# Order of the gate and up parts, and where the expert loop reads its bounds: a mixture-of-experts kernel on one core

## The reference, cut to what matters

```python
x = x + xattn(layernorm(x), ctx, ctx, mask, ...)
h = layernorm(x)                            # 2048 tokens x 256
shared = (silu(h @ gw) * (h @ uw)) @ dw     # 256 -> 512 -> 256
logits = h @ gate_w                         # 2048 x 32
id = argmax(logits); score = sigmoid(max(logits))
xs = (h * score)[argsort(id)]               # tokens sorted by expert
g = ragged_dot(xs, routed_gate_w, tokens_per_expert)
u = ragged_dot(xs, routed_up_w, tokens_per_expert)
d = ragged_dot(silu(g) * u, routed_down_w, tokens_per_expert)
out = x + shared + d[inverse order]
```

## Time and profile before

| | |
|---|---|
| median of 3 executions | 301.97 us (300.6 to 305.56) |
| the profiled execution, its own time | 302.95 us |
| its span | 301.0 us |
| granted TensorE clock, mean | 0.98 |
| PE busy | 255.7 us (85%) |
| DVE, ACT, POOL busy | 154.7, 94.2 and 88.5 us |
| HBM read, written | 59.49 MB, 8.91 MB |
| the expert loop, first to last gate matmul | 131.0 to 265.5 us |
| its gate and up matmuls (L1022) | 2528, 89.9 us busy |
| its down matmuls (L1044) | 1264, 50.5 us busy |

### The profile page before, as it was taken

How to read it: one execution, slowest core, us unless ns; L and a number is a source line. 1 busy time by engine, 2 the same in 40 slices (tenths; PEclk the granted TensorE clock), 3 DMA queues, 4 the chain that set the end, 5 groups by cost and what they waited for, 6 DMA issues and landing times.

```text
span 301.0 us, 13003 instructions
## 1 busy us (share of the span) xinstructions
PE 255.7 (85%) x4627; PEld 181.5 (60%) x4629; DVE 154.7 (51%) x490; ACT 94.2 (31%) x284; POOL 88.5 (29%) x248
## 2 busy tenths in 40 slices
PE   4977899998798999979797999899899899799710
PEld 3745656653383468747676787777787677553600
DVE  0538867884399341135454555555455455433423
ACT  2048766533121011433232333333233333212000
POOL 1245211111007766012122222222222222102772
PEclk9999999999799999999999999999999999999995
DMA  6999994000001234406989499999999999924565
GB/s 197 340 371 373 375 371 174 0 3 2 0 0 71 105 107 139 139 2 217 337 288 306 154 349 315 346 382 382 375 375 383 382 374 374 316 56 106 166 210 164
DMA packets 53040, 68.69 MB, mean 228 GB/s; under 512 B 3967, under 2 KB 35100, under 8 KB 53020
## 3 DMA queue, kind: packets, MB, share of 16 engines
q1 hardware_dynamic: 46203, 61.60, 59.1%
q0 software_dynamic: 1536, 4.20, 4.5%
q10 hardware_dynamic: 5280, 2.62, 3.4%
HBM read 59.49 MB, written 8.91 MB: 227 GB/s over the span
## 4 chain that ended last, share of the span: by engine, by line
PE 66%; DVE 9%; DMA 7%; issue 7%; POOL 5%; ACT 4%; POOLq 1%; ACTq 1%; SPq 0%; DVEq 0%
PE bank L1022 25%; PE bank L947 14%; PE bank L1044 12%; PE bank L959 5%; POOL xs_flat L463 4%; DMA ring_gu<-n_L_ffn_routed_up_w_dram 3%; PE bank L878 3%; DMA slot_rows<-late 2%; DVE h_place L531 1%; PE bank L913 1%; DVE h_place L532 1%; ACT h_place L746 1%; DMA h_place<-in_L_xattn_kernel_q_dram 1%; DMA xs_flat<-slot_rows,slot_i 1%; PE bank L896 1%
## 5 line engine op out<-in xcount | busy, mean ns | idle before, releaser
L1022 PE MATMUL bank<-ring_gu,x_c 128*32 128x128 f32 x2528 | 89.9, 276 | 9.7 <-issue 6.1
L1022 PEld LDWEIGHTS bank<-ring_gu,x_c 128*32 128x32 f32 x2528 | 64.0, 109 | 28.0 <-issue 15.7
L1044 PE MATMUL bank<-ring_d,h_place 128*32 128x128 f32 x1264 | 50.5, 274 | 3.9 <-issue 0.8
L644 DVE TENSOR_TENSOR h_place<-h_place,bank 128x128 f32<-128x128 f32 x79 | 22.7, 288 | 48.8 <-ACT h_place L781 48.8
L456 POOL COPY x_c<-xs_flat 128x32 f32 x79 | 16.7, 212 | 97.2 <-PE bank L1022 84.7
L1044 PEld LDWEIGHTS bank<-ring_d,h_place 128*32 128x32 f32 x1264 | 35.1, 109 | 11.5 <-issue 10.6
L781 ACT ACTIVATE h_place<-bank 128x128 f32<-128x128 f32 x79 | 21.9, 278 | 46.4 <-PE bank L1022 45.3
L786 ACT COPY late<-bank 128x128 f32 (+1 forms) x79 | 21.0, 266 | 45.3 <-PE bank L1044 45.3
L648 DVE STREAM_TRANSPOSE h_place<-h_place 128x128 f32<-128x128 f32 x79 | 24.6, 312 | 13.5 <-PE bank L1044 8.3
L959 PE MATMUL bank<-shd,h_place 128*128 128x256 f32 x128 | 28.4, 380 | 2.1 <-DVE h_place L532 2.1
L531 DVE SCALAR_TENSOR_TENSOR h_place<-h_place,bank 128x512 f32<-128x512 f32 x16 | 11.0, 686 | 34.0 <-ACT h_place L746 34.0
(11 more groups left out here) (132 smaller groups left out, 251.2 us busy)
## 6 DMA issues: line engine op xcount, KB each, us to landing
ring_gu<-L_ffn_routed_gate_w_dram SPq DMA_DIRECT2D x32, 512.0 KB, 8.9
ring_gu<-n_L_ffn_routed_up_w_dram SPq DMA_DIRECT2D x32, 512.0 KB, 10.1
ring_d<-L_ffn_routed_down_w_dram SPq DMA_DIRECT2D x32, 512.0 KB, 10.2
slot_rows<-late ACTq DMA_DIRECT2D x10, 256.0 KB, 5.9
x<-in_x_dram SPq DMA_DIRECT2D x4, 512.0 KB, 7.0
slot_rows<-zeros SPq DMA_DIRECT2D x1, 2048.0 KB, 14.3
late<-sorted_rows SPq DMA_DIRECT2D x8, 256.0 KB, 3.2
out_dram<-x SPq DMA_DIRECT2D x8, 256.0 KB, 2.4
```

Source lines behind the costliest of these rows:

```text
L644: v.tensor_tensor(h_r, g_silu, bank[1][:, 0:P], ALU.mult).then_inc(h_ready, 1)
L1022: ins = te.matmul(bank[g][q * LW:(q + 1) * LW, 0:P].rearrange("p (m f) -> p m f", f=LW), x_c[:, k], columns[:, q], start=(k == 0), stop=(k ...
L1044: ins = te.matmul(bank[2][r:r + LW, 0:DH], hT[:, f * LW:(f + 1) * LW], ring_d[:, s, f, a * DH:(a + 1) * DH], start=(m == 0), stop=(m == HA ...
```

## The change

Three things. In `gate_up` both gate parts come first, so that `g_done` is counted after the second part and not after the third; up's first part, with `x0_used` behind it, is now the third, and its wait for `h_ready` goes with it. The wait for half 1 of the tokens (`x1_part`) comes ahead of the second part rather than the third. The tables `turn_end` and `turn_first` become one table `turn` of unsigned 16-bit values, read without a check of bounds. And the round is rotated: the first chunk of the next expert stands at the end of an expert's piece, so that the loop over rounds is entered with a first chunk already done and with its number and end carried in two registers. `turn_first` and the `If` are gone.

```diff
-        turn_first = sb("turn_first", [1, NE], I32)
-        turn_end = sb("turn_end", [1, NE], I32)
+        turn = sb("turn", [1, NE + 1], U16)
...
-            v.tensor_scalar(turn_end[:], chunk_cum[0:1], 1.0, None, ALU.add).then_inc(table_ready, 1)
-            v.scalar_tensor_tensor(out=turn_first[:], in0=chunk_cum[0:1], scalar=1.0, in1=chunk_f[0:1],
-                                   op0=ALU.add, op1=ALU.subtract).then_inc(table_ready, 1)
+            v.memset(turn[:, 0:1], 1).then_inc(table_ready, 1)
+            v.tensor_scalar(turn[:, 1:NE + 1], chunk_cum[0:1], 1.0, None, ALU.add).then_inc(table_ready, 1)
...
                 part(0, 0)
+                pe.wait_ge(x1_part, w)
+                part(0, 1).then_inc(g_done, 1)
                 pe.wait_ge(h_ready, w)
                 part(1, 0).then_inc(x0_used, 1)
-                pe.wait_ge(x1_part, w)
-                part(0, 1).then_inc(g_done, 1)
                 part(1, 1).then_inc(u_done, 1)
...
-            def expert(w, e, s, before, landed):
-
-                pe.wait_ge(gu_in[s], 2 * landed)
-                gate_up(w, s)
-                end = pe.value_load(turn_end[0:1, bass.ds(e, 1)], min_val=2, max_val=MAX_CHUNKS + 1)
-                if before is None:
-                    with pe.If(it > 0):
-                        down_of(w, RING - 1)
-                else:
-                    down_of(w, before)
+            def turn_of(e):
+                return nc.values_load(turn[0:1, bass.ds(e, 1)], engines=(mybir.EngineType.PE,), min_val=1, max_val=MAX_CHUNKS + 1,
+                                      skip_runtime_bounds_check_because="unsigned, a running sum of chunks with at least one for each expert")
+
+            def other_chunks(w, end, s, landed):
+
                 pe.wait_ge(d_in[s], landed)
                 with pe.If(w + 1 < end):
                     with pe.Fori(w + 1, end) as more:
                         gate_up(more, s)
                         down_of(more, s)
                     pe.nop()
-                return end
-
+
+            def next_expert(w, e, s, landed):
+
+                n = (s + 1) % RING
+                pe.wait_ge(gu_in[n], 2 * landed)
+                gate_up(w, n)
+                end = turn_of(e + 2)
+                down_of(w, s)
+                return w, end
...
+            pe.wait_ge(gu_in[0], 32)
+            gate_up(1, 0)
+            carry(1, turn_of(1))
             with pe.Fori(0, ROUNDS) as it:
-                w = pe.value_load(turn_first[0:1, bass.ds(RING * it, 1)], min_val=1, max_val=MAX_CHUNKS)
+                w, end = carried()
                 for s in range(RING):
-                    w = expert(w, RING * it + s, s, s - 1 if s else None, 16 * it + 16)
-            w = pe.value_load(turn_first[0:1, RING * ROUNDS:RING * ROUNDS + 1], min_val=1, max_val=MAX_CHUNKS)
+                    other_chunks(w, end, s, 16 * it + 16)
+                    w, end = next_expert(end, RING * it + s, s, 16 * it + (16 if s + 1 < RING else 32))
+                carry(w, end)
+            w, end = carried()
```

More of the change, by code:

```diff
@@ L12 @@
 U32 = mybir.dt.uint32
+U16 = mybir.dt.uint16
 P = 128
@@ L1066, in expert, with carried, carry @@
                     pe.nop()
-                return end
+            def next_expert(w, e, s, landed):
[5 more added lines that the diff above has]
+                return w, end
+            first_turn = pe.alloc_register("first_turn")
+            first_end = pe.alloc_register("first_end")
+            def carried():
+                return (pe.snap(first_turn, min_val=1, max_val=MAX_CHUNKS),
+                        pe.snap(first_end, min_val=2, max_val=MAX_CHUNKS + 1))
+            def carry(w, end):
+                pe.reg_mov(first_turn, w)
+                pe.reg_mov(first_end, end)
+            pe.wait_ge(gu_in[0], 32)
+            gate_up(1, 0)
+            carry(1, turn_of(1))
             with pe.Fori(0, ROUNDS) as it:
-                w = pe.value_load(turn_first[0:1, bass.ds(RING * it, 1)], min_val=1, max_val=MAX_CHUNKS)
+                w, end = carried()
                 for s in range(RING):
-                    w = expert(w, RING * it + s, s, s - 1 if s else None, 16 * it + 16)
-            w = pe.value_load(turn_first[0:1, RING * ROUNDS:RING * ROUNDS + 1], min_val=1, max_val=MAX_CHUNKS)
+                    other_chunks(w, end, s, 16 * it + 16)
+                    w, end = next_expert(end, RING * it + s, s, 16 * it + (16 if s + 1 < RING else 32))
+                carry(w, end)
+            w, end = carried()
             for s in range(REST):
-                w = expert(w, RING * ROUNDS + s, s, s - 1 if s else RING - 1, 16 * ROUNDS + 16)
+                other_chunks(w, end, s, 16 * ROUNDS + 16)
+                if s + 1 < REST:
+                    w, end = next_expert(end, RING * ROUNDS + s, s, 16 * ROUNDS + 16)
             down_of(n_chunks + 1, REST - 1)
```

## The result

| | before | after |
|---|---|---|
| median of 20 runs each, us | 301.95 (300.6 to 305.56) | 300.2 (297.96 to 307.17) |
| ratio | | 0.9932, 95% interval 0.9907 to 0.9958 |
| profiled execution, us | 302.95, span 301.0 | 298.73, span 296.8 |
| loop's first load of gate, us into the span | 130.96 | 130.04 |
| SyncE issues expert 12's gate | 171.70 | 168.89 |

The medians differ by 1.75 us (0.6%), the ratio gives 0.7%. The forecast was 295.8 and the range began at 292.5 and ended at 300.0; the time lies just above it.

A forecast was written before the change was run, and what follows sets the result against it. TensorE's freeing of ring places bounds the loop's first half, the weight stream the second. Savings of 4.7, 2.1 and 0.3 us, taken as 7.0, gave 295.95 for the profiled execution, 295.0 at the median, stated as 295.8; range 292.5 to 300.

The forecast's parts named there:

- Expert 4's, without the pause inside it: First chunk of expert 4 in the loop's first half: saves 0.6 us, its 1.76 us pause staying as it is.
- the instruction pause moves: Rival, chance 0.12: the 1.76 us mid-chunk pause may not occur in code of another length, giving 294 us.
- expert 12's gate 4.7 us earlier: Sum of TensorE's savings up to the 23rd chunk, for which SyncE waits: expert 12's weights land 4.7 us earlier.
- the last up weights 6.8 earlier: End of the loop's weight stream: 4.7 us from the first half plus 2.1 us of stream pauses recovered.
- Chunks inside an expert: Chunks behind another of their expert take 1.35 us; eight of fifteen save 0.10 each, 0.8 us in all.
- the copies come late: Rival, chance 0.17: POOL's half 0 is released a part later, every chunk pays up to 0.13 us more: 298 us.
- First chunks of experts 1 to 3: First chunks of 1.96, 1.89 and 1.87 us become 1.46 through the unchecked read, saving 1.3 us.
- The ends of the round: Rotated round, at experts 5 and 6: two first chunks of 3.36 and 1.88 us become 1.53 and 1.96, saving 1.75.
- The first silu: Start of the loop: the first silu starts a part earlier and the 2nd chunk waits for it, saving 0.2 us.
- the pauses of the stream behind expert 12's gate: Transfers from 171.0 to 191.6 us: of 2.8 us of pauses waiting for experts 7 and 8, 2.1 go.
- the 17 us that TensorE alone would save: TensorE's savings over 79 chunks, about 17 us, ten of them waited away in the stream-bound second half.
- the clock's rival: Chance 0.05: TensorE's clock falls to half while it waits in the second half, slowing the last twelve experts: 311 us.

The follow-up runs named there:

- e6: Changed kernel with the ring's first refill of weights held until the 12th chunk's up is done: 305.29 us, ratio 1.0164 to the kernel before.
- e10: Kernel before with only expert 7's refill held until the 9th chunk's up is done: 300.44 us, ratio 0.9959.
- e13: Changed kernel with only expert 7's refill held until the 9th chunk's up is done, repeated on another chip: 298.03 us, ratio 0.9867.
- e15: Changed kernel with signed 32-bit values and checked reads, and expert 7's refill held until the 9th chunk's up is done: 300.22 us, ratio 0.993.
- e11: Changed kernel with signed 32-bit values and the check of each read kept, no refill held: 304.8 us, ratio 1.0082 to the kernel before.
- held to 12: First refill of the ring held until the 12th chunk's up is done: 305.29 us in the changed kernel, 308.54 us in the kernel before.
- e9: Changed kernel with only expert 7's refill held until the 9th chunk's up is done: 297.77 us, ratio 0.9861 to the kernel before.
- e14: Kernel before, unaltered, measured and profiled again: 302.92 us, ratio 1.0023.
- e1: Kernel before with only gate's parts moved ahead of up's parts: 301.68 us, ratio 0.9971.
- e16: Changed kernel, unaltered, measured again for comparison: 300.54 us, ratio 0.9942 to the kernel before.

## Why the prediction was wrong

**The step that failed** is the one in the sum over the first half: "Expert 4's, without the pause inside it (1.76, kept as it is): 0.6." I took the pause for a length that TensorE pays, as if it were an instruction's duration. It is a wait for something that arrives at a time of its own, the packet of code, and that time is set by the weights in flight: with the DMA engines kept free it starts 13.4 to 14.9 us into the loop and the stop goes (e6 to e10, e13, e15), with the full stream 16.2 to 17.7, and 19.1 in e11. So what TensorE gains ahead of such a point turns into a longer stop. Chunk 10 did not save 0.6 but lost 1.04 us. The 0.6 was right for what it left out: with both kernels held to 12, where neither stops, the chunk takes 0.54 us less. Of my rivals "the instruction pause moves" came nearest, but it asked if other code has the pause and not what the pause waits for.

The hold shows what the rest of the sum was worth. I had expert 12's gate 4.7 us earlier, which is 171.7 - 4.7 - 131.0 = 36.0 us into the loop, and the last up weights 6.8 earlier, 125.1 into it. With the stop out of the way they are at 35.0 and 125.3 (e9), 35.4 and 126.4 (e13). Part of that is luck: it takes in the 1.76 us of pause that I had kept, and the 0.5 us of POOL's read. And the time does not follow: e9 and e13 take 297.8 and 298.0 us, still 2.0 and 2.2 over the 295.8, so the stop is not the whole of the miss. Between the two held kernels, e10 and e9, the change gives 3.6 us up to expert 12's gate and 3.8 up to the last landing.

**The 4.7 term by term.** Measured 1.9 (168.89 - 130.04 against 171.70 - 130.96), 2.8 less:
- expert 4's first chunk: forecast -0.6, measured +1.04: 1.6 of the 2.8.
- Chunks inside an expert: forecast 0.8 us for eight of them, measured 0.2 over all. Most took 1.34 to 1.36 as I had it, but three took 1.42 to 1.47, released by POOL's L456, and two of expert 6's took 1.57 and 1.98, where they had 1.58 and 1.92. The rival "the copies come late" was right in these few and wrong in the rest: 0.6.
- First chunks of experts 1 to 3: 1.65, 1.50 and 1.60 for 1.96, 1.89 and 1.87: 0.97 for 1.3. The ends of the round (experts 5 and 6): 1.48 for 1.75. Together 0.6.
- The first silu: 0.22 for 0.2.

**Right in the mechanism:** the pauses of the stream behind expert 12's gate gave 1.8 us for 2.1 (91.1 us from that issue to the last landing became 89.3). Waits ahead of down other than the stop vanished, waits for L644 vanished, inside an expert chunks mostly come 1.34 to 1.36 apart, a later expert's first chunk takes 1.49 for the forecast 1.46, and TensorE waits for up weights ahead of most experts from the 24th on, 7.3 us of its matmuls and 8.9 of its loads for the forecast 10. Of the 17 us that TensorE alone would save, the stream takes the larger part: the change is worth 11.2 us with a lighter stream and 0.3 to 1.8 with the full one. That part of the argument carried, though two of its signs did not come: expert 12's gate was issued at 168.9 for 167.0, and two slices behind 172 us were at 336 and 344 GB/s, where none was to be under 370.

**The sum for the profiled execution** was 6.8 and 0.3, 7.1 us; the prediction took 7.0, to 295.95. Measured are 4.2: 0.9 from the stretch ahead of the loop, which no step of mine explains, 1.9 and 1.8, less 0.4 behind the last landing. Two smaller slips don't touch the forecast: the chances that the prediction adds up to 0.45 make 0.40 (0.25, 0.12 and 0.03), and the last twelve experts have 22 chunks and not 25, so that the clock's rival was priced some 5 us too high.

**The clock.** It falls once in the loop, to 0.50 (1.2 GHz), from 254.3 to 257.7, directly behind the 2.71-us wait for the weights of an expert that follows one of a single chunk:

```profile
254.30:257.70 3.40, 3.40 (x74) 3.39 (x67) 0.88 (x3) 0.70 (x3) 0.43 (x2) 0.50 1.05 375
249.90:254.00 4.10, 1.43 (x48) 1.16 (x48) 0.93 (x4) 0.54 (x2) 0.43 (x2) 1.00 1.06 373
```

Two chunks then take 2.15 and 2.16 us, and the next starts at 258.35, 0.15 behind the landing that it would have waited for. I had put this at "a single fall is waited away", and so it was. A fall behind the stop is not: in e14, e1 and e11 the clock fell to 0.50 for 3.4 us right behind the stop at expert 4, and chunk 11 took 2.2 to 2.4 us for 1.34. In none of the changed kernel's four profiled executions did it fall there.

```profile
150.40:153.80 3.40, 3.40 (x72) 3.19 (x68) 1.11 (x4) 0.55 (x2) 0.52 (x3) 0.50 1.06 389
```

(That is e14.) The Trainium skill (TensorE: Matmul & The Clock Gate, section "HAM oscillation — how this bites in real kernels") has bursts with transfer waits between them throttle the array again and again. In the changed kernel's loop, with five waits of 0.3 to 2.2 us for weights ahead of the one of 2.71, it was one fall, and it cost nearly nothing.

**What stays open.** The profiled executions gain 4.2 us (or, by e14 and e16, 5.0), the medians of the four sets 0.3 to 1.8. The profiled execution of the changed kernel lay under its own median in all four sets (by 1.5, 2.4, 1.6 and 2.2 us), that of before above it in both (1.0 and 0.4). Since other executions leave no records, I can't say what they lose. Where on an engine a packet of code waits, and why it came 0.4 to 1.4 us later into the loop in the changed kernel than in before, and in e11 1.4 to 2 us later still, was not tried.

## What to carry to other kernels

A stop without a releaser in the first pass through unrolled code may be an arrival, not a duration: look when the packets of kind "instruction" start, and against what traffic. If it is one, work saved ahead of it can be worth nothing, and holding one transfer for a few us, at a place where the stream has pauses anyway, can be worth more than the edit. Where one stream bounds the later half, count only what the faster engine gives back to the stream's gaps, and carry the estimate to the median with care: one profiled execution of each kernel differed by more than twice what the medians did.

## What the runs showed of the hardware

- Code for TensorE comes in packets of 16 KB on the DMA engines that move the weights. In the first round of the loop they start 4.4 to 5.2 us apart on empty engines (e6) and 5.9 to 8.2 under the stream (before and after), each taking about 1 us; between 162 and 262 us, the later rounds, before has none. The Trainium skill (Runtime: NRT & Kernel Launch, section "Instruction fetch mechanics") says that the sequencer fetches the next 16 KB block by a DMA queue of its own while it works on the present one, and that the cost of crossing a block is mostly hidden. The size agrees; the cost does not where the engines are full: a stop of 1.8 and 1.9 us in before, 3.0 to 3.6 in the changed kernel and 4.1 in e11, and 0.3 and 0.5 where the engines were kept free for that packet (e9, e13).
- The check of a value read by TensorE's sequencer costs 0.3 us at each expert and about 2 us in all where the stop is out of the way (e15 to e13), also when the value is not needed until the next expert. The sequencer does it in order: in e11 the loads of down behind it wait with "issue" 31 times, 11.2 us in all, and in the changed kernel once.
- 16 bits instead of 32 shorten the read by little: 288 ns for 306.
- Right behind a stop of 1.9 to 4.1 us TensorE's granted clock was 0.50 for 3.4 us in e1, e11 and e14; behind the seven other stops of 1.8 us and more (before 1.76, the changed kernel 3.0 to 3.6) it stayed at 1.00.
